# Splitting each mix-matrix strip product of a one-core Trainium2 kernel into two products of 64 output rows in two column tiles

## The chip, the cores and the metric

The kernel runs on one core of one Trainium2 chip. The metric is the device time of one execution in microseconds (us); lower is better. TensorE (PE) does the matrix products, VectorE (DVE), ScalarE (ACT) and GpSimd (POOL) the rest; DMA transfers are issued mostly by SyncE (SP).

## What is computed

The reference is one transformer-like block on 2048 tokens of 1024 features, all float32. Cut to what matters here:

```python
# first half: a mix matrix, kept only where a sparse mask is 1
attn = einsum('ds,td->st', w1, w2) * sparse_mask     # w1, w2, mask: 1024 x 1024
y    = gelu(einsum('bds,st->bdt', x, attn) + b2)
x    = layernorm(x + y)
# second half: weights decoded from bit planes with a 16-entry table per row
x    = layernorm(x + x @ dequant(qweight, lut4).T + bias)   # an 8-bit variant for rows of large norm
```

The mask is 1 only near the diagonal: six-wide windows, shifted by 0, 32 and 64, and their transpose. So of each block of 128 output rows of `attn` only the block itself and at most 69 columns on either side can be nonzero. The kernel rounds that to `REACH = 72` columns.

## The kernel before

**The mix matrix.** The 1024 rows of `attn` are eight blocks `b` of 128. For each block the kernel computes a strip of at most 128 x 272 entries (72 + 128 + 72; 200 columns for the first and the last block, which have only one side) into a PSUM bank, as a sum over eight contraction blocks `d` of 128. The operands `w1` (stationary, 128 columns) and `w2` (moving, up to 272 columns) are plain float32. `strip_row(b, d)` issues one such product; there are 64.

**What is used of a strip.** VectorE's `mask_strip(b)` multiplies the strip by the mask. It takes the middle 128 columns on all 128 rows, the left 72 columns on rows 0 to 63 only and the right 72 columns on rows 64 to 127 only (lines 948, 950 and 953). The few entries beyond that are computed separately by `excess_strip` (line 436), a 48-column product.

**Order.** Each engine runs its instructions in the order written, and semaphores tie the engines together. TensorE does nine warm-up products, then `front_strips()` (`d` outside, blocks 0 to 3 inside), then `back_strips(0)` (blocks 4 and 5) and `back_strips(1)` (blocks 6 and 7). SyncE loads `w1` and `w2` in nine pieces in the same order, and TensorE waits for a piece where it first reads it: five pieces for the front (`d` = 0, 1, 2-3, 4-5, 6-7), then two halves (`d` = 0-3, 4-7) for each pair of back blocks. SyncE waits for nothing in these loads; the masks, the first tokens and part of the bit planes lie between them in its queue.

**What follows.** After the strips TensorE applies the mix matrix to the tokens, group by group (512 tokens): `own(g, t)` is three 512-column products of a diagonal block (lines 475 to 477), `beside(g, t)` three pairs for the blocks beside it, each pair working on partitions 0 to 63 and 64 to 127 (lines 500 and 502), and `excess(g, pair)` (line 487) adds the remaining entries. `own(0, 0)` waits for `make_x_lo(0, 0)` on VectorE (line 1005), and `excess_strip()` is issued after `own(0, 1)`. VectorE's `make_mix_e` (lines 974 to 986) waits for that strip.

VectorE and ScalarE meanwhile decode the weights of the second half (`decode_step`). In VectorE's program the order near the strips' end is `make_x_lo(0, 0)`, `make_x_lo(0, 1)`, `mask_strip(6)`, `make_mix_lo(4)`, `mask_strip(7)`, `make_mix_lo(5)`, `make_mix_e()`. The remaining 240 us are the rest of the first half and the products of the second half (lines 571 to 573).

Of the kernel before, what the change touches and what calls it, by code (L numbers as in the profile page):

```python
# [6 lines left out]
P = 128  # L7
# [6 lines left out]
SIDE = P // 2  # L14
SPAN = STRIDE * (STRIPES - 1)
BITS = 8
REACH = -(-(SPAN + WINDOW - 1) // BITS) * BITS
# [21 lines left out]
def post_ln_block(nc, xt, xr, xe_in, w1d, w1e, w2d, w2e, b2c, mask, mask_b, mask_e, mask_rest, qbits, lut4, lut8, bias, out):  # L39
# [4 lines left out]
    GROUPS, KB = xt.shape[0], xt.shape[1]  # L44
    D = KB * P
# [55 lines left out]
    with ctx:  # L101
# [7 lines left out]
        def at(name, kib, shape, dt):  # L109
            return nc.alloc_sbuf_tensor_at(name, [P] + shape, dt, offset=origin + int(kib * KIB))  # L110
# [3 lines left out]
        w2 = at("w2", 32, [KB, D], f32)  # L114
        w1 = at("w1", 64, [KB, D], f32)
# [71 lines left out]
        def unit_bank(t):  # L187
            return acc[:, UNIT_BANKS[t], :]
# [70 lines left out]
        def strip_of(b):  # L259
            return max(b * P - REACH, 0), min((b + 1) * P + REACH, D)  # L260

        def places_of(b):
            first, end = strip_of(b)
            return slice(first - b * P + REACH, end - b * P + REACH)
# [161 lines left out]
        def _(pe):  # L426
# [11 lines left out]
                last.then_inc(e_made, 1)  # L438

            def strip_row(b, d):  # L440
                first, end = strip_of(b)
                return nc.tensor.matmul(unit_bank(b)[:, places_of(b)], w1[:, d, b * P:(b + 1) * P], w2[:, d, first:end],  # L442
                                        start=d == 0, stop=d == KB - 1)

            def front_strips():
                starts = [first for first, _ in ROW_PIECES]
                for d in range(KB):
                    if d in starts:
                        pe.wait_ge(w_loaded[starts.index(d)], 32)
                    for b in range(FRONT):  # L450
                        last = strip_row(b, d)
                        if d == KB - 1:
                            last.then_inc(mix_made, 1)

            def back_strips(n):
                for d in range(KB):
                    if d % HALF_BLOCKS == 0:
                        pe.wait_ge(w_loaded[len(ROW_PIECES) + 2 * n + d // HALF_BLOCKS], 32)
                    for b in (FRONT + 2 * n, FRONT + 2 * n + 1):
                        last = strip_row(b, d)  # L460
                        if d == KB - 1:
                            last.then_inc(mix_made, 1)
# [184 lines left out]
            with nc.tensor.If(wanted > 0):  # L647
                with pe.Fori(0, KB) as b:
                    with pe.Fori(0, KB) as t:
                        pe.wait_ge(g_w_lo, KB * b + t + 1)  # L650
                        for d in range(KB):
# [3 lines left out]
                            last = nc.tensor.matmul(acc[:, 0, 0:P], lo, g_w_hi[:, 1, d, :], start=False,  # L655
                                                    stop=d == KB - 1)
# [980 lines left out]
```

## Time and profile before

| | |
|---|---|
| median of 3 runs | 298.35 us (298.05 to 298.6) |
| the profiled execution, its own time | 298.25 us |
| its span from the first to the last instruction | 296.4 us |
| TensorE busy in the span | 281.9 us, 95% |
| VectorE busy | 217.9 us, 73% |
| ScalarE busy | 195.7 us, 66% |
| mean granted TensorE clock | 0.99 |
| strip products (line 442) | 64 products, 128 matmul records, from 5.1 to 35.6 us |

How to read it: the profiled execution took 298.25 us from outside, and 296.4 us lie between its first and last instruction. A float32 product leaves two matmul records, each with a weight load of its own, so the 64 strip products are 128 records. The time of one record is a latency, as matmuls are pipelined and their ends are modelled; what a product costs the engine is the distance from one start to the next.

### The profile page before, as it was taken

The page shows a single profiled execution, that of the slowest core. Times are in us where ns is not written, and L with a number is a line of the kernel's source. Part 1 is how long each engine was busy: PE and PEld are TensorE (multiplying, and loading weights), DVE is VectorE, ACT ScalarE, POOL GpSimd, SP SyncE. Part 2 cuts the span into 40 slices and gives each one's busy share as a digit, 9 for nine tenths or more (in the row PEclk, how much of TensorE's full clock was granted, in tenths as well). Part 3 has the DMA queues.
Part 4 walks back from the last instruction along what each step waited for, and adds up shares of the span by engine and source line. Part 5 has one row for each costly group of instructions (what it writes and reads, how often), then busy time and mean ns, then how long its engine had stood idle before and what let it go on. Part 6 is the DMA issues. An engine that isn't in the chain of part 4 may idle for free.

```text
span 296.4 us, 4898 instructions
## 1 busy us (share of the span) xinstructions
PE 281.9 (95%) x1835; PEld 245.8 (83%) x1835; DVE 217.9 (73%) x355; ACT 195.7 (66%) x257; POOL 88.5 (30%) x152
## 2 busy tenths in 40 slices
PE   8899989899999999999999999999999999999980
PEld 4688866667668999999999999999988778888880
DVE  1679999897868977997979686295578586763371
ACT  2866368988999979989989985362447446222110
POOL 4000001533353202121520000000387866766421
PEclk9999999999999999999999999999999999999995
DMA  6999999999999611111111111174188663434323
GB/s 211 400 358 358 377 376 333 246 247 243 205 196 195 138 35 53 38 35 55 35 56 35 45 45 38 54 160 197 64 260 287 226 212 141 140 115 155 123 114 111
DMA packets 28479, 49.76 MB, mean 168 GB/s; under 512 B 2464, under 2 KB 11936, under 8 KB 28448
## 3 DMA queue, kind: packets, MB, share of 16 engines
q1 hardware_dynamic: 23392, 40.53, 40.1%
q0 software_dynamic: 4352, 8.39, 15.8%
q10 hardware_dynamic: 704, 0.46, 0.5%
q8 instruction: 16, 0.26, 0.4%
q14 instruction: 15, 0.12, 0.1%
HBM read 36.79 MB, written 12.58 MB: 167 GB/s over the span
## 4 chain that ended last, share of the span: by engine, by line
PE 60%; ACT 8%; DVE 8%; SPq 7%; DMA 6%; POOL 5%; issue 5%; DVEq 0%; ACTq 0%
PE acc L571 14%; PE acc L573 14%; PE acc L572 14%; PE acc L500 4%; DMA w<-in_w2d 3%; PE acc L475 2%; SPq L286 2%; ACT leaf L745 2%; ACT zz L788 2%; PE acc L510 2%; PE acc L476 2%; PE acc L477 2%; DMA off_band<-in_mask_rest 2%; SPq L285 1%; DVE leaf L1032 1%
## 5 line engine op out<-in xcount | busy, mean ns | idle before, releaser
L571 PE MATMUL acc<-lin,zz 128*128 128x256 f32 (+2 forms) x424 | 130.6, 308 | 0.3 <-issue 0.3
L573 PE MATMUL acc<-lin,zz 128*128 128x256 f32 (+2 forms) x424 | 129.8, 306 | 0.0
L572 PE MATMUL acc<-lin,zz 128*128 128x256 f32 (+2 forms) x424 | 129.5, 306 | 0.0
L571 PEld LDWEIGHTS acc<-lin,zz 128*128 128x128 f32 x424 | 80.1, 189 | 4.5 <-issue 0.5
L572 PEld LDWEIGHTS acc<-lin,zz 128*128 128x128 f32 x424 | 80.2, 189 | 3.9
L573 PEld LDWEIGHTS acc<-lin,zz 128*128 128x128 f32 x424 | 80.0, 189 | 4.1
L745 ACT ACTIVATE leaf<-planes,lut,flip 128x1024 f32<-128x1024 uint8 x56 | 67.5, 1236 | 1.2 <-DVE dest L1032 1.2
L1032 DVE COPY_PREDICATED leaf<-planes,leaf 128x1024 f32<-128x1024 uint8 x32 | 43.5, 1360 | 14.0 <-ACT leaf L745 13.3
L1493 POOL DMA_DIRECT2D z<-in_xr x16 | 19.5, 1224 | 70.8 <-ACT z L727 68.2
L854 ACT ACTIVATE junk<-rows,cols 128x1024 bf16<-128x1024 f32 x15 | 17.2, 1146 | 35.1 <-POOL cols L1467 35.1
L1032 DVE COPY_PREDICATED dest<-planes,leaf 128x1024 f32<-128x1024 uint8 x24 | 32.5, 1356 | 3.7 <-ACT leaf L745 2.3
L442 PE MATMUL acc<-w,w 128*128 128x272 f32 (+1 forms) x128 | 29.3, 389 | 1.2 <-DMA w<-in_w2d 1.2
L442 PEld LDWEIGHTS acc<-w,w 128*128 128x128 f32 x128 | 24.2, 196 | 6.6 <-DMA w<-in_w2d 2.8
L1465 POOL TENSOR_TENSOR cols<-cols 128x1 f32<-128x1 f32 x15 | 6.8, 455 | 67.0 <-DVE rows L1152 66.9
L1074 DVE TENSOR_TENSOR zz<-z,zz 128x1024 fp32r<-128x1024 f32 x16 | 19.3, 1222 | 7.6 <-ACT zz L788 7.6
L1152 DVE SCALAR_TENSOR_TENSOR rows<-acc,cols,bias_bc 128x512 f32<-128x512 f32 x15 | 11.2, 750 | 17.1 <-PE acc L573 16.9
L727 ACT ACTIVATE z<-acc,b 128x512 f32<-128x512 f32 x32 | 20.3, 692 | 4.2 <-PE acc L502 4.2
L1443 POOL TENSOR_SCALAR cols<-parts 128x1 f32<-128x1 f32 x16 | 9.7, 609 | 41.3 <-ACT parts L838 41.3
L838 ACT ACTIVATE parts<-acc 128x258 f32<-128x258 f32 (+1 forms) x32 | 12.1, 377 | 12.8 <-PE acc L573 12.7
L1005 DVE TENSOR_TENSOR x_lo<-z,x_hi 128x1024 fp32r<-128x1024 f32 x16 | 19.0, 1222 | 0.3
L1157 DVE TENSOR_SCALAR rows<-rows,cols 128x1024 f32<-128x1024 f32 x15 | 12.2, 813 | 8.9 <-POOL cols L1474 8.8
L843 ACT ACTIVATE off_band<-off_band 128x896 f32<-128x896 f32 x8 | 7.6, 952 | 15.1 <-DMA off_band<-in_mask_rest 15.1
(118 smaller groups left out, 438.4 us busy)
## 6 DMA issues: line engine op xcount, KB each, us to landing
z<-in_xt SPq DMA_DIRECT2D x16, 512.0 KB, 8.7
z<-in_xr POOLq DMA_DIRECT2D x16, 512.0 KB, 8.5
out_rows<-rows SPq DMA_DIRECT2D x15, 512.0 KB, 2.9
out_rows<-parts SPq DMA_DIRECT2D x32, 128.0 KB, 1.7
rows<-out_rows SPq DMA_DIRECT2D x16, 256.0 KB, 2.7
w<-in_w1d SPq DMA_DIRECT2D x7, 512.0 KB, 9.0
off_band<-in_mask_rest SPq DMA_DIRECT2D x8, 448.0 KB, 4.7
w<-in_w2d SPq DMA_DIRECT2D x3, 584.0 KB, 9.5
```

The lines of the kernel that those rows point to most:

```text
L442: return nc.tensor.matmul(unit_bank(b)[:, places_of(b)], w1[:, d, b * P:(b + 1) * P], w2[:, d, first:end], start=d == 0, stop=d == KB - 1)
L571: nc.tensor.matmul(bank, hi, w_hi, start=k == 0, stop=False)
L572: nc.tensor.matmul(bank, hi, w_lo, start=False, stop=False)
L573: last = nc.tensor.matmul(bank, lo, w_hi, start=False, stop=k == KB - 1)
L727: nc.scalar.activation(z[:, g, t, :], unit_bank(t), ACT.Gelu, bias=b2[:, t:t + 1]).then_inc(gelu_done, 1)
L745: nc.scalar.activation(to, planes[:, b % 2, 0, :], ACT.Identity, bias=lut[:, b, 2 * i:2 * i + 1], scale=flip[:, b, i:i + 1]).then_inc(leaf ...
L854: nc.scalar.activation(junk[:, :], rows[:, j % 4, :], ACT.Square, bias=neg_mean2[:, j:j + 1], accum_out=sq2[:, j:j + 1]).then_inc(squared2, 1)
L1005: nc.vector.tensor_tensor(x_lo[:, 2 * r:2 * r + 2, :], z[:, g, 2 * r:2 * r + 2, :], x_hi[:, 2 * r:2 * r + 2, :].bitcast(f32), ALU.subtract ...
L1032: nc.vector.copy_predicated(to, planes[:, b % 2, plane, :], leaf[:, other, :]).then_inc(merged, 1)
L1074: nc.vector.tensor_tensor(zz[:, 0, g, 2 * r:2 * r + 2, :], z[:, g, 2 * r:2 * r + 2, :], zz[:, 1, g, 2 * r:2 * r + 2, :].bitcast(f32), ALU. ...
L1157: nc.vector.tensor_scalar(rows[:, j % 4, :], rows[:, j % 4, :], neg_mean2[:, j:j + 1], rstd2[:, j:j + 1], ALU.add, ALU.mult).then_inc(norm ...
L1493: nc.gpsimd.dma_start(z[:, g, 2 * r:2 * r + 2, :], xr[g, 2 * r:2 * r + 2].rearrange("k p n -> p k n"), accum_op=ALU.add).then_inc(residual ...
```

## The change

`strip_row` issues two products where it issued one. The first has the weight columns 0 to 63 of the block, writes PSUM partitions 0 to 63, and streams the block's own 128 columns and the 72 to the left. The second has weight columns 64 to 127, writes partitions 64 to 127, and streams the own 128 columns and the 72 to the right. The output partitions place them in the two 64-column tiles of the 128-column array. The corner regions that no longer are computed (rows 64 to 127 of the left 72 columns, rows 0 to 63 of the right 72) are those that `mask_strip` does not read.

```diff
             def strip_row(b, d):
-                first, end = strip_of(b)
-                return nc.tensor.matmul(unit_bank(b)[:, places_of(b)], w1[:, d, b * P:(b + 1) * P], w2[:, d, first:end],
-                                        start=d == 0, stop=d == KB - 1)
+                for rows_, low, high in ((slice(0, SIDE), REACH, 0), (slice(SIDE, P), 0, REACH)):
+                    first, end = max(b * P - low, 0), min((b + 1) * P + high, D)
+                    to = unit_bank(b)[rows_, first - b * P + REACH:end - b * P + REACH]
+                    half = w1[:, d, b * P + rows_.start:b * P + rows_.stop]
+                    last = nc.tensor.matmul(to, half, w2[:, d, first:end], start=d == 0, stop=d == KB - 1)
+                return last
```

The order of TensorE's program shows it. In the rows below `acc` is the PSUM, `w_51` and `w_52` are the two weight matrices in SBUF, the size is output partitions by streamed columns, and `w_loaded5` to `w_loaded8` are the landings of the last four pieces of the weights. First `back_strips(0)` and the start of `back_strips(1)` in the kernel before:

```order
 L442 MATMUL acc<-w_51,w_52 128x272 [waits w_loaded5]
 L442 MATMUL acc<-w_51,w_52 128x272 x7
 L442 MATMUL acc<-w_51,w_52 128x272 [waits w_loaded6]
 L442 MATMUL acc<-w_51,w_52 128x272 x7
 L442 MATMUL acc<-w_51,w_52 128x272 [waits w_loaded7]
 L442 MATMUL acc<-w_51,w_52 128x200
```

The same place in the changed kernel:

```order
 L445 MATMUL acc<-w_51,w_52 64x200 [waits w_loaded5]
 L445 MATMUL acc<-w_51,w_52 64x200 x15
 L445 MATMUL acc<-w_51,w_52 64x200 [waits w_loaded6]
 L445 MATMUL acc<-w_51,w_52 64x200 x15
 L445 MATMUL acc<-w_51,w_52 64x200 [waits w_loaded7]
 L445 MATMUL acc<-w_51,w_52 64x200 x2
 L445 MATMUL acc<-w_51,w_52 64x128
```

The eight products behind each landing have become sixteen, and the two halves of a product stand one behind the other. Then the end of the strips on the same engine, where `own(0, 0)`, `own(0, 1)` and `excess_strip` follow, in the kernel before:

```order
 L442 MATMUL acc<-w_51,w_52 128x200
 L475 MATMUL acc<-x_hi,mix_hi 128x512 [waits x_lo_made,mix_lo]
 L476 MATMUL acc<-x_lo,mix_hi 128x512
 L477 MATMUL acc<-x_hi,mix_lo 128x512
 L475 MATMUL acc<-x_hi,mix_hi 128x512 [waits x_lo_made,mix_lo]
 L476 MATMUL acc<-x_lo,mix_hi 128x512
 L477 MATMUL acc<-x_hi,mix_lo 128x512
 L436 MATMUL acc<-w_e 128x48 [waits masked,e_ld]
```

And in the changed kernel, where lines after the edit are 3 higher:

```order
 L445 MATMUL acc<-w_51,w_52 64x200 x3
 L445 MATMUL acc<-w_51,w_52 64x128
 L478 MATMUL acc<-x_hi,mix_hi 128x512 [waits x_lo_made,mix_lo]
 L479 MATMUL acc<-x_lo,mix_hi 128x512
 L480 MATMUL acc<-x_hi,mix_lo 128x512
```

What follows the strips waits for the same semaphores as before, and nothing but the strips' own products has changed. In all there are 128 strip products instead of 64, 112 of 200 columns and 16 of 128.

## Rows read from the trace of the kernel before

**Rows 1.** The page: span, TensorE's busy time, and the chain that ended last, by engine.
```profile
span 296.4 us, 4898 instructions
PE 281.9 (95%) x1835; PEld 245.8 (83%) x1835; DVE 217.9 (73%) x355; ACT 195.7 (66%) x257; POOL 88.5 (30%) x152
...
PE 60%; ACT 8%; DVE 8%; SPq 7%; DMA 6%; POOL 5%; issue 5%; DVEq 0%; ACTq 0%
```

**Rows 2.** The chain that ended last, 20 to 45 us: start, us, what.
```profile
22.28 9.81 DMA w<-in_w2d
...
32.13 3.46 PE acc L442 x16
...
37.00 1.73 PE acc L436 x16
```

**Rows 3.** Timeline of TensorE: start, us to the last end, records, idle before.
```profile
5.86 1.11 PE L442 MATMUL acc<-w,w 128*128 128x272 f32 x2
...
7.20 0.62 PE L442 MATMUL acc<-w,w 128*128 128x272 f32 x2
...
10.76 0.60 PE L442 MATMUL acc<-w,w 128*128 128x200 f32 x2 [0.86 <-DMA w<-in_w2d]
...
12.57 0.50 PE L442 MATMUL acc<-w,w 128*128 128x200 f32 x2
...
20.68 0.62 PE L442 MATMUL acc<-w,w 128*128 128x272 f32 x2
...
32.13 3.46 PE L442 MATMUL acc<-w,w 128*128 128x272 f32 x16 [0.31 <-DMA w<-in_w2d]
```

**Rows 4.** Loads of weights: the chain's issue rows, and DMA windows holding one issue each.
```profile
5.34 0.60 SPq L279
...
w<-in_w2d SPq DMA_DIRECT2D x1, 584.0 KB, 11.1
...
17.62 2.30 SPq L286
...
w<-in_w2d SPq DMA_DIRECT2D x1, 368.0 KB, 9.4
```

**Rows 5.** Timeline of VectorE, 20 to 40 us.
```profile
20.54 0.37 DVE L948 TENSOR_TENSOR mix_raw<-acc,band 128x128 f32<-128x128 f32 x1 [0.95 <-DMA band<-in_mask_b]
...
34.00 2.36 DVE L1005 TENSOR_TENSOR x_lo<-z,x_hi 128x1024 fp32r<-128x1024 f32 x2
...
38.04 0.40 DVE L960 TENSOR_TENSOR mix_lo<-mix_raw,mix_hi 128x256 fp32r<-128x256 f32 x1
38.76 0.26 DVE L974 TENSOR_TENSOR raw_e<-acc,band_e 128x96 f32<-128x96 f32 x1 [0.32 <-PE acc L436]
```

**Rows 6.** All waits of VectorE, 20.9 to 40 us: total, times, longest.
```profile
DVE mix_raw L948 <- DMA band<-in_mask_b: 1.0, 1, 1.0
DVE raw_e L974 <- PE acc L436: 0.3, 1, 0.3
```

**Rows 7.** Groups of TensorE and its weight loads, 0 to 75 us, shapes apart: busy us, mean ns.
```profile
L442 PE MATMUL acc<-w,w 128*128 128x272 f32 x96 | 25.2, 401 | 0.3 <-DMA w<-in_w2d 0.3
...
L436 PE MATMUL acc<-w_e 128*128 128x48 f32 x16 | 1.9, 271 | 0.0
...
L442 PEld LDWEIGHTS acc<-w,w 128*128 128x128 f32 x128 | 24.2, 196 | 6.6 <-DMA w<-in_w2d 2.8
```

**Rows 8.** Timeline of TensorE, 61 to 66 us: pairs on partitions 0-63 and 64-127.
```profile
61.51 0.40 PE L500 MATMUL acc<-x_hi,mix_lo 64*128 64x512 f32 x1
61.51 0.39 PE L502 MATMUL acc<-x_hi,mix_lo 64*128 64x512 f32 x1
61.75 0.39 PE L500 MATMUL acc<-x_hi,mix_hi 64*128 64x512 f32 x1
```

**Rows 9.** The chain that ended last, 61 to 66 us, across a change of tiling.
```profile
62.60 0.43 PE acc L475
63.03 0.23 PE acc L476
```

## The prediction

> **What bounds the kernel now.** I read the page first. The last-ended chain is 60% TensorE, and TensorE is busy for 95% of the span [rows 1]: a microsecond lost on it early is likely lost for good. Whether one gained early is kept must be read where the strips end, so next came the chain from 20 to 45 us [rows 2]. It does not run through the strips of the front. It runs through SyncE's queue to the last piece of `w2`, issued at 22.28 and landed at 32.09 us, then through the 16 records behind that piece (3.46 us), `own` and the 16 records of `excess_strip` to `make_mix_e`. The reader is to see that transfers, not products, set when the last quarter of the strips may start.
>
> Third, TensorE's timeline [rows 3]. Before the last piece TensorE waited only 0.31 us (it was busy to 31.82), and before the piece landing at 10.7 us it waited 0.86 us. In between it was dense. So strips and transfers are nearly balanced: faster strips run into landings, much slower ones soon move the end.
>
> Fourth, VectorE [rows 5, 6]. From 20.9 to 38.4 us it does not wait for a strip at all; its first `mask_strip` waited for the mask's transfer (to 20.54), and it waits for TensorE only once, 0.32 us at 38.76, for `excess_strip`. `make_x_lo(0, 0)`, which `own(0, 0)` needs, is the first half of the pair from 34.00 to 36.36, so it ends near 35.2.
>
> **What a product costs now.** Two 272-column records at 20.68 cover 0.62 us; less one record's latency (0.39, [rows 7] has a mean of 0.401) their starts are 0.229 apart. For 200 columns: 0.50 - 0.33 = 0.169 [rows 3]. Difference: 0.060 us for 72 columns, 0.83 ns a column; so a record is 0.0025 + 0.00083 x columns. With two records a product: 272 columns 0.458 us, 200 columns 0.338, 128 columns 0.218. Behind the last landing stand four products of 272 and four of 200: 4 x (0.458 + 0.338) = 3.19 us, and a restart after the wait of about 0.10 (32.13 + 3.46 less the last latency 0.33 gives the last start, 35.26; the 15 steps make 3.02 of the 3.13 between). So the strips leave the engine at 32.13 + 0.10 + 3.19 = 35.42.
>
> **The change, part by part.**
>
> *Streams.* An inner block's 0.458 becomes two products of 0.338 on different halves of the array. No row of this kernel shows column tiles. Bounds: from below, they run at once and a block costs 0.338; from above, one after the other, 0.677. The nearest rows are the `beside` pairs [rows 8]: two records on partitions 0-63 and 64-127 start in the same 10 ns, and the next pair 0.24 later, the price of one. Those are row tiles of one record each. Here a half has two records, A1 A2 B1 B2 in program order. If starts are in order and a tile holds one stream, B1 starts with A2, and B2 with the next A1: four records in two slots of 0.169. I take 0.338, since the overlap of tiles is the nearest row. The end blocks cost 0.338 either way (200 and 128 columns at once), as before. The Trainium skill, TensorEngine Tiling (Array Packing), Key Properties, says that tiles can load and multiply in parallel, and TensorE: Matmul & The Clock Gate, Part 3, gives 2.38 times for three column tiles; no run here shows it.
>
> *Weight loads.* 128 loads become 256 of half the columns. The dearest price in sight is that of `excess_strip`, whose 48-column records are too short to hide a load: 1.73 us for 16 [rows 2], 0.108 each. Four at full price would be 0.43 a block, four at half price 0.22. Now 128 loads (24.2 us busy) lie under products of the same 128 rows, for the starts are 0.229 apart with loads of 0.196 [rows 7]. I take them as hidden, cost 0; if their price does not halve, the cover of 0.338 is gone and a block costs 0.43.
>
> *Change of tiling.* After pairs of 64 rows, the first record of 128 rows takes 0.43 us in the chain, the next 0.23 [rows 9]: 0.20 for the change. One is added on the path, strips to `own(0, 0)`; the one from warm-up to strips lies ahead of landings TensorE waits for anyway.
>
> *The sum.* At once, front blocks cost 4 x 0.338 = 1.35 a `d`. The front's last piece lands at 5.34 + 11.1 = 16.4 [rows 4], so the front ends at 16.4 + 2.7 = 19.1, still ahead of the mask at 20.5 for which VectorE waits. The third back piece lands at 17.62 + 9.4 = 27.0; its eight products end at 27.0 + 8 x 0.338 = 29.7. The last piece lands at 32.1 as before, since SyncE issues it behind no engine. Then 32.13 + 0.10 + 2.71 = 34.94, 0.48 earlier than 35.42. But `own(0, 0)` needs its tokens at 35.2, so it starts then, with a change of tiling that lies partly under the wait: first stream at about 35.2 to 35.4, a gain of 0 to 0.2, say 0.1. Nothing behind can return more, as VectorE's slack at `excess_strip` is 0.32 and its program is dense to 38.44. So 5.8 us less of TensorE work (48 blocks x 0.12) is worth 0.1 us. Sum: 298.25 - 0.1 = 298.15; the profiled execution was 0.1 below the median of 298.35, so the forecast is 298.2.
>
> **The rivals.**
>
> *Halves do not overlap.* In favour: no row shows two records of one product's kind at once, each half brings two records of its own tile in a row, and both tiles read the same 128 partitions, where the row tiles each read their own 64. Against: [rows 8]. Then inner blocks cost 0.677 and end blocks 0.338 + 0.218 = 0.556. TensorE falls behind from the second piece on: the first `d` at the early half rate (two 272-column records at 5.86 cover 1.11 us, starts 0.45 apart, 0.23 from 7.2 on, [rows 3]) ends near 8.7, the second 2.59 later at 11.3; then 6 x (0.556 + 3 x 0.677) = 15.5 to 26.8, back blocks 4 and 5 16 x 0.677 = 10.8 to 37.6, blocks 6 and 7 8 x (0.677 + 0.556) = 9.9 to 47.5, with the tiling change 47.7: 12.3 later than 35.42. VectorE, dense but only 18 us of work after the first mask, is done earlier, so all of it shows: 298.35 + 12.3 = 310.6. This is the rival on the other side; it decides from about 0.468 a block on (from 10.76 + 0.10, 56 blocks of cost c must end by 35.4, 14 of them end blocks and 0.12 cheaper each: 56c - 1.7 = 24.5), and every 0.01 beyond costs 0.56 us.
>
> *Weight loads become the bound.* Four of 0.108, 0.43 for every block, the end blocks too: 32.23 + 8 x 0.43 = 35.7, with the change of tiling 35.9, 0.45 later: 298.8, at the edge of what can be told. For: double the loads; against: they have half the columns.
>
> *Loads that can't lie under products.* Then 0.338 + 0.43 = 0.77 a block: 10.86 + 56 x 0.77 = 54.0, plus 0.2, 18.8 later: 317. Against it speaks that 0.196 us loads already hide. The page TensorE: Matmul & The Clock Gate of the Trainium skill, Part 3, says that a weight load overlaps products in flight only when its row group differs, and two column tiles share theirs; the trace of before disagrees for this kernel, as its loads of all 128 rows hide.
>
> *The clock falls.* At once, TensorE would stand idle from 29.7 to 32.1, 2.4 us, where its longest pause among the strips is now 0.86 [rows 3], and the mean granted clock of the span is 0.99. If the lower level (1.2 of 2.4 GHz) came back, 0.45 against 0.229 a record, the last eight products would cost 5.4 instead of 2.7 and end at 37.6, with the tiling change 37.8: 2.4 later, 300.7. For: the strips start at that level, in spite of the nine warm-up products ahead of them. Against: a pause of 0.86 did nothing.
>
> **How the numbers follow.** At once, loads hidden, clock kept: 0.60. Load-bound: 0.07. Clock: 0.06. No or little overlap: 0.24. Exposed loads: 0.03. The likeliest has its own range of 297.8 to 298.7: the gain can't pass 0.3, to which the run's spread of 0.3 is added. A change of 0.2%, 0.6 us, is what a measurement of this kernel can tell from none. Same: nearly all of the first case and half of the load-bound one, 0.58; faster by more 0.05, if something is freed that I don't see; slower 0.37. The range must reach the case without overlap, as it holds over 2 in 10: 297.8 to 311.0; it leaves out only the exposed loads.
>
> **What would show it.** Right: 256 strip records, 128 starts of them beside another, mean distance 0.085 us; TensorE idle before the second to fourth back pieces, above all about 2.4 us before 32.1; `own(0, 0)` within 0.2 us of before; VectorE's program unmoved. Wrong: starts 0.169 apart without idle time and strips that end near 47 us; starts 0.11 apart (loads); records twice as far apart after 32.1 (clock); or a last landing that is not at 32.1. The forecast fails outright if column tiles don't overlap with two-record float32 products; a partial overlap up to 0.468 a block would leave it standing.

## The result and the profile after

The changed kernel took 299.5 us (median of 19 runs, 298.52 to 301.31), the kernel before 298.7 (19 runs, 297.97 to 299.8): 0.8 us slower between the medians. The ratio of the means is 1.003 (0.9 us) with a 95% interval of 1.0017 to 1.0043. The profiled execution took 299.01 us. The forecast was 298.2 and "same" the likeliest.

The page of the changed kernel, against [rows 1]: TensorE has 6 us less to do, and the span is 0.8 us longer.

```profile
span 297.2 us, 5154 instructions
PE 275.8 (93%) x1963; PEld 240.8 (81%) x1963; DVE 218.0 (73%) x355; ACT 195.6 (66%) x257; POOL 88.6 (30%) x152
...
PE 58%; DVE 11%; ACT 8%; DMA 6%; POOL 5%; issue 5%; SPq 3%; DVEq 0%; ACTq 0%
```

**The halves do overlap.** TensorE's timeline after, against [rows 3]; the columns are those of [rows 3].

```profile
20.91 0.85 PE L445 MATMUL acc<-w,w 128*64 128x200 f32 x8
...
28.28 2.53 PE L445 MATMUL acc<-w,w 128*64 128x200 f32 x28
32.82 2.92 PE L445 MATMUL acc<-w,w 128*64 128x200 f32 x32 [2.01 <-DMA w<-in_w2d]
36.58 0.47 PE L478 MATMUL acc<-x_hi,mix_hi 128*128 128x512 f32 x1 [0.83 <-DVE x_lo L1008]
```

The 28 records from 28.28 cover 2.53 us; less one latency of 0.33 that is 2.20 for 13 steps of 0.169, two records a step (the row of eight at 20.91 gives 0.52 for three). So a block of four records costs 0.338 us. The 32 records behind the last piece take 2.92 us where 16 took 3.46. The price on which the forecast rested is right.

**But the end of the strips came later.** The last piece landed at 32.8, not at 32.1, TensorE had stood idle for 2.01 us, and `own(0, 0)` started at 36.58 instead of 35.4, because it waited for VectorE's `make_x_lo`. VectorE's timeline and all its waits say why, against [rows 5] and [rows 6]:

```profile
21.73 0.38 DVE L951 TENSOR_TENSOR mix_raw<-acc,band 128x128 f32<-128x128 f32 x1 [2.03 <-DMA band<-in_mask_b]
...
35.21 2.36 DVE L1008 TENSOR_TENSOR x_lo<-z,x_hi 128x1024 fp32r<-128x1024 f32 x2
...
39.96 0.26 DVE L977 TENSOR_TENSOR raw_e<-acc,band_e 128x96 f32<-128x96 f32 x1 [0.32 <-PE acc L436]
```

The first `mask_strip` started at 21.73 instead of 20.54, and every VectorE instruction from there to `raw_e` is 1.19 to 1.23 us later than before. This is the whole shift: TensorE's wait for VectorE, the wait at `raw_e` (0.32 in both) and the groups behind it keep their distances. It lasts: SyncE issues the last store at 291.86 us instead of 290.56, 1.30 later. Of that 0.8 is left in the span, so in this pair of profiles the end behind the last store took 0.5 us less. The reader is to see that the lateness enters at one instruction, which waits for the mask transfer and for nothing of TensorE's.

**Why the mask was late.** Three views: transfers from 18.0 to 18.1 us of the changed kernel, transfers from 24.6 to 24.8 us of the kernel before, and the mask's own issue, after and before (us from issue to landing in the last column).

```profile
q1 hardware_dynamic: 31, 0.04, 113.4%
q8 instruction: 1, 0.02, 72.4%
```
```profile
q1 hardware_dynamic: 80, 0.06, 109.6%
q8 instruction: 1, 0.02, 37.2%
```
```profile
band<-in_mask_b SPq DMA_DIRECT2D x1, 400.0 KB, 11.2
```
```profile
band<-in_mask_b SPq DMA_DIRECT2D x1, 400.0 KB, 10.2
```

Beside the data the DMA engines carry the instructions: a packet of 16 KB on queue 8. By the packets' own records it starts at 24.66 us and takes 1.19 us before, and starts at 18.05 us and takes 1.16 us after. A transfer lands in 16 parts. Those of the mask, from the landing records (us):

```
before  15 from 19.26 to 20.42, the last 20.52
after   15 from 19.39 to 20.51, the last 21.70
```

Fifteen parts are in time, one is late by the length of the read. The same happens to the small transfer of the bit planes (15 by 20.94, one at 22.14) and holds up SyncE's queue (the issue at 17.71 takes 3.46 us, 2.30 before), and the pieces of the weights behind the read land late too (20.65, 25.14, 27.75 and 32.78 against 19.43, 23.91, 26.99 and 32.09). That the last piece is late because of the read is read from these times; no run tests it alone. Before, the read came behind the mask's landing.

### The profile page after: what moved, and what is told of

Same layout as the page of the kernel before. It is cut to its first block, busy times and chain, and to the rows that moved or that the text cites. A ratio compares the mean times of both kernels' runs of the same rounds, so it can differ in the third digit from the quotient of the medians.

```text
span 297.2 us, 5154 instructions
## 1 busy us (share of the span) xinstructions
PE 275.8 (93%) x1963; PEld 240.8 (81%) x1963; DVE 218.0 (73%) x355; ACT 195.6 (66%) x257; POOL 88.6 (30%) x152
## 4 chain that ended last, share of the span: by engine, by line
PE 58%; DVE 11%; ACT 8%; DMA 6%; POOL 5%; issue 5%; SPq 3%; DVEq 0%; ACTq 0%
PE acc L574 14%; PE acc L576 14%; PE acc L575 14%; DMA band<-in_mask_b 4%; PE acc L503 4%; PE acc L478 2%; ACT leaf L748 2%; DVE leaf L1035 2%; ACT zz L791 2%; PE acc L513 2%; PE acc L479 2%; PE acc L480 2%; DMA off_band<-in_mask_rest 2%; PE acc L557 1%; DVE dest L1035 1%
## 5 line engine op out<-in xcount | busy, mean ns | idle before, releaser
L445 PE MATMUL acc<-w,w 128*64 128x200 f32 (+1 forms) x256 | 23.3, 329 | 7.6 <-DMA w<-in_w2d 7.5
L445 PEld LDWEIGHTS acc<-w,w 128*64 128x64 f32 x256 | 19.3, 137 | 11.8 <-DMA w<-in_w2d 10.5
L1077 DVE TENSOR_TENSOR zz<-z,zz 128x1024 fp32r<-128x1024 f32 x16 | 19.3, 1224 | 7.7 <-ACT zz L791 7.7
```

The source lines that it names most:

```text
L445: last = nc.tensor.matmul(to, half, w2[:, d, first:end], start=d == 0, stop=d == KB - 1)
L1077: nc.vector.tensor_tensor(zz[:, 0, g, 2 * r:2 * r + 2, :], z[:, g, 2 * r:2 * r + 2, :], zz[:, 1, g, 2 * r:2 * r + 2, :].bitcast(f32), ALU. ...
```

## The experiments

Each run also has a mean granted clock, and these told more than one profile. The changed kernel: 7 of 19 runs at 0.990 or more, with a median of 298.89; 12 at 0.982 to 0.986, with 299.89. The kernel before, beside the experiments: 30 of 35, 28 of 35 and 23 of 29 runs at 0.990 or more, with medians of 298.68, 298.60 and 298.37. So the profiled execution shows one cause, and most runs have a second.

What the mean says must be read from the clock records of the profiles. In each of them the clock is at its lower level from 290 to 295 us to the end, for 2.9 to 6.0 us; this alone makes a mean of 0.990 to 0.995. Four of the 13 profiles hold one more stretch at the lower level, each 3.41 us long, which takes another 0.006. So a run at 0.986 or less very likely lost the clock somewhere before the end, and one at 0.987 to 0.989 may or may not have. The mean does not say where the clock fell.

Two theories, which may add up: the instruction read moves ahead of the mask; the granted clock falls behind the pause of 2 us. The rival to both: column tiles or the change of tiling cost something by themselves.

All eleven kernels had 12 runs each; "high" counts those at 0.990 or more, "low" those at 0.986 or less. By the same count the changed kernel had 12 of 19 low, and the kernel before 0 of 35, 0 of 35 and 2 of 29. The runs came from three chips, and the changed kernel itself was not run again beside them, so a comparison with its 299.5 or 298.89 is one across sessions; the high runs of the kernel before alone differ by 0.3 us between them.

| run | median us | before, same chip | ratio (95%) | high | median of high | low |
|---|---|---|---|---|---|---|
| after_warm1 | 299.38 | 298.68 | 1.0018 (1.0000 to 1.0036) | 3 | 298.66 | 6 |
| before_tiny25 | 298.71 | 298.68 | 0.9995 (0.9976 to 1.0013) | 11 | 298.69 | 0 |
| after_band_first | 298.86 | 298.68 | 0.9999 (0.9971 to 1.0027) | 3 | 298.40 | 5 |
| split_back_only | 300.49 | 298.68 | 1.0060 (1.0035 to 1.0085) | 2 | 298.13 | 7 |
| after_fill | 298.98 | 298.64 | 1.0000 (0.9980 to 1.0019) | 12 | 298.98 | 0 |
| split_back_fill | 300.72 | 298.64 | 1.0065 (1.0035 to 1.0095) | 4 | 299.57 | 5 |
| split_back_band_fill | 298.61 | 298.64 | 1.0005 (0.9984 to 1.0026) | 10 | 298.57 | 0 |
| before_narrow | 299.15 | 298.64 | 1.0018 (0.9990 to 1.0046) | 6 | 298.39 | 5 |
| before_tiny44 | 298.85 | 298.38 | 0.9995 (0.9972 to 1.0019) | 12 | 298.85 | 0 |
| after_band_fill | 298.69 | 298.38 | 1.0012 (0.9978 to 1.0046) | 8 | 298.36 | 3 |
| split_back_fill8 | 298.60 | 298.38 | 0.9997 (0.9971 to 1.0023) | 9 | 298.29 | 1 |

**after_warm1**, to move the read back:

```diff
-    WARM_UP = 9
+    WARM_UP = 1
```

> The changed kernel with 1 warm-up product instead of 9, so TensorE's program reaches every later point 8 products sooner. Theory (instruction read): in the changed kernel a 16 KB packet of the instruction queue starts at 18.05 us, takes 1.16 us, and one of the 16 parts of the mask transfer lands at 21.70 while the other 15 are in by 20.51; VectorE is late by 1.20 us from there to the end. With 8 products fewer ahead of it the read should start behind the front's 64 products, after 20 us, the mask should land at 20.5, and the time should be 0.9 to 1.3 us below the changed kernel, at about the kernel before. Rival (transfers vary by themselves, or the column tiles slow them): the mask still lands near 21.7 and the time is that of the changed kernel. Rival (the 1.2 us come from the change of tiling or a lower clock): no gain, and a loss if fewer warm-ups lower the clock of the front.

A miss on where the read falls: it started at 18.13, and the first `mask_strip` at 21.11. Eight bf16 warm-up products are too few instructions to move it past the front. But its profile, at a mean clock of 0.985, caught the second cause. The windows of this run (the columns are the length, TensorE, its weight loads, VectorE, ScalarE and GpSimd busy, then the granted clock, the share of the DMA engines and GB/s):

```profile
30.00:32.00 2.00, 0.17 (x2) 0.00 (x0) 1.96 (x9) 0.68 (x2) 0.00 (x0) 1.00 1.12 368
32.00:34.00 2.00, 1.71 (x13) 1.59 (x15) 1.92 (x6) 1.42 (x4) 0.00 (x0) 0.63 1.01 376
34.00:36.00 2.00, 2.00 (x17) 1.74 (x14) 1.97 (x3) 0.92 (x1) 0.00 (x0) 0.51 1.06 392
36.00:38.00 2.00, 2.00 (x15) 1.47 (x12) 1.92 (x5) 0.25 (x1) 0.00 (x0) 1.00 1.08 362
```

TensorE stands idle from 30 to 32.3 us; then the granted clock is at the lower of its two levels (1.2 of 2.4 GHz) until about 36, and the last 32 records take 4.60 us instead of 2.92. `own(0, 0)` starts at 36.82 and `raw_e` at 40.23, 1.47 later than in the kernel before; 0.57 of this is the late mask, so the fallen clock cost 0.9 us. The Trainium skill, TensorE: Matmul & The Clock Gate, in its part on HAM oscillation, says that waits for transfers between bursts of products bring the half rate back. This trace agrees, after a wait of 2.12 us; the profiles of `after`, `after_band_first`, `split_back_only` and `before_narrow` have waits of 2.0 to 2.1 us at the same place and no fall behind them.

**before_tiny25**, to pull the read forward in a kernel without column tiles:

```diff
-    WARM_UP = 9
+    WARM_UP = 4
...
+            for _ in range(25):
+                nc.tensor.matmul(acc[:, SUM_BANK, 0:8], warm[:, 0:P], warm[:, 0:8], start=True, stop=True)
```

> The kernel before with 4 warm-up products and 25 products of 8 columns instead of 9 warm-up products: 20 more products in TensorE's program, the strips untouched. Theory (instruction read): the read that starts at 24.66 us in the kernel before is pulled ahead of the mask's landing at 20.5, one part of the mask lands about 1.2 us late, VectorE's first mask_strip starts near 21.7, and the kernel is about 1.2 us slower (0.4%) without any column tile. Rival (column tiles or faster strips are the cause): the mask lands at 20.5 and the time is that of the kernel before within 0.2%.

A miss: the read moved from 24.66 to 20.36, still too late to touch the mask (20.54 in both), and the time stayed. It shows that the length of TensorE's program places the read, and that added products cost nothing by themselves.

**after_band_first**, to take the mask out of the read's way:

```diff
-            load_back(0, 0)
             load_band(0)
+            load_back(0, 0)
```

> The changed kernel with the first mask half (band) loaded ahead of the first back piece of the weights instead of behind it. Theory (instruction read): the mask lands near 17.5 to 18.7, so the read no longer delays VectorE's first mask_strip, which starts when the decode step ahead of it is done, near 19.7; but the read still delays the later transfers, so the last piece of weights lands near 32.8, the strips end near 35.6, and own(0, 0) starts near 35.8 instead of 36.6: 0.6 to 1.0 us faster than the changed kernel, about the kernel before. Rival (the 1.2 us arise in the strips themselves): nothing changes.

As expected by the read: the first `mask_strip` starts at 19.35, `own(0, 0)` at 35.17, `raw_e` at 38.60 (39.96 in the changed kernel, 38.76 in the kernel before), and the median is 0.6 us below the changed kernel's and 0.2 above that of before on its chip. The last piece came at 32.3, better than expected. Only 3 of 12 runs kept the high clock. One of the other nine took 452.59 us at a mean clock of 0.558; it is not in the ratio, and it has no trace.

The profiled execution (299.36 us, 0.989) lost its clock, but not behind the pause of 2.06 us ahead of the last piece. Its windows (columns as above):

```profile
243.00:244.00 1.00, 1.00 (x5) 0.74 (x4) 1.00 (x2) 0.62 (x1) 0.95 (x1) 0.54 0.73 252
244.00:245.00 1.00, 1.00 (x4) 0.80 (x3) 1.00 (x2) 1.00 (x3) 0.00 (x0) 0.50 0.99 401
```

The store that SyncE issues at 242.77, as in the kernel before (242.72), is the last in time; the one that came at 254.64 comes at 256.21. So a fall here costs 1.5 us. TensorE had been idle for 0.87 us ahead of 240.72 (0.64 in the kernel before, whose clock stayed, and 0.90 in before_tiny44, whose clock stayed too).

**split_back_only**, one part of the change alone:

```diff
+                if b < FRONT:
+                    first, end = strip_of(b)
+                    return nc.tensor.matmul(unit_bank(b)[:, places_of(b)], w1[:, d, b * P:(b + 1) * P], w2[:, d, first:end],
+                                            start=d == 0, stop=d == KB - 1)
```

> Only the products of blocks 4 to 7 are split; blocks 0 to 3 are whole as in the kernel before. Theory (instruction read): TensorE's program ahead of the first back piece is that of the kernel before, so the read starts no earlier than that piece's landing at 19.5, at 20 to 21 us; the mask lands at 20.5 and the time is within 0.1% of the kernel before, perhaps 0.1 us faster, unless the read just touches the mask's last part (then up to 1.2 us slower). Rival (column tiles cost on the path, as the change of tiling ahead of own(0, 0)): as slow as the changed kernel, 0.9 us above before.

The read starts at 25.22, the mask lands at 20.44, and the two runs at 0.990 take 298.04 and 298.21 us, like before. The ten others take 300.8 in the median. So a run with a fallen clock is 2.7 us slower here and 1.0 in the changed kernel. This is the larger effect, which I had not expected of this run. Why it is larger is open, as no such run of this kernel was profiled. In the changed kernel VectorE's lateness of 1.2 us could hide part of a fall behind the last piece; but such a fall made the strips only 1.7 us longer in after_warm1, less than the 2.7 here, so more than that is in these ten runs. A fall near 243 us (1.5 us in after_band_first) and the late store of split_back_fill below are candidates.

**after_fill**, to take away the pause alone:

```diff
+            def fill(pairs, alone):
+                for _ in range(pairs):
+                    for rows_ in (slice(0, SIDE), slice(SIDE, P)):
+                        nc.tensor.matmul(unit_bank(KB - 1)[rows_, 288:488], w1[:, 0, rows_], w2[:, 0, 0:200],
+                                         start=alone, stop=alone)
...
                 for d in range(KB):
+                    fill({(1, 4): 6}.get((n, d), 0), d == 0)
```

> The changed kernel with six more pairs of 64-row products (2.0 us of TensorE work, into unused columns of a bank) ahead of the wait for the last piece of the weights, in the pause of 2.1 us. Theory (clock): in most executions of the changed kernel the granted clock halves behind that pause; with the pause filled the mean clock should be 0.99 or more in nearly all runs, their time about that of the changed kernel's runs at 0.99 or more (298.9), so 0.5 to 0.9 us below its median of 299.5. What the instruction read costs stays, 0 to 0.4 us above before. Rival (the read alone makes the 0.9 us): the time stays 299.5, with the clock as before.

All 12 runs kept 0.990 or more, against 7 of 19, and the median is 298.98: 0.5 below the changed kernel's and near that of its high runs (298.89). Against the kernel before on the same chip the ratio is 1.0000, where it was 1.003. TensorE's timeline shows the filled pause (line 461 is the filler):

```profile
30.23 2.31 PE L461 MATMUL acc<-w,w 128*64 128x200 f32 x23
32.57 2.92 PE L445 MATMUL acc<-w,w 128*64 128x200 f32 x32
36.27 0.47 PE L485 MATMUL acc<-x_hi,mix_hi 128*128 128x512 f32 x1 [0.78 <-DVE x_lo L1015]
```

More work on TensorE made the kernel faster. The fillers also change the places of the later reads (one at 227.02 instead of 232.86), so that the pause alone made the difference is likely, not shown. The wait for `x_lo` of 0.78 us, which the read causes (at 18.74, first `mask_strip` at 21.42), is left, and so are 0.3 us against before by the medians (298.64).

**before_narrow**, the same speed of the strips without a column tile and without one instruction more. The right 72 columns of the inner strips are left incomplete from the second contraction block on.

```diff
                 first, end = strip_of(b)
-                return nc.tensor.matmul(unit_bank(b)[:, places_of(b)], w1[:, d, b * P:(b + 1) * P], w2[:, d, first:end],
+                if d and 0 < b < KB - 1:
+                    end -= REACH
+                to = unit_bank(b)[:, first - b * P + REACH:end - b * P + REACH]
+                return nc.tensor.matmul(to, w1[:, d, b * P:(b + 1) * P], w2[:, d, first:end],
```

> The kernel before with whole 128-row products, but the inner blocks stream only 200 columns from the second contraction block on; the right 72 columns of their strips are left incomplete. So a product costs 0.338 us as in the changed kernel, with no column tile and not one instruction more. Theory (clock): the same pauses as in the changed kernel, so the clock falls below 0.99 in more than half of the runs and the median is 0.3 to 2 us above before, while the instruction read starts at 24 us or later and the mask lands at 20.5. Rival (column tiles or the added instructions are the whole cause): clock and time as before, or 0.1 us faster.

TensorE's timeline has the same pause ahead of the last piece:

```profile
27.24 3.09 PE L445 MATMUL acc<-w,w 128*128 128x272 f32 x16 [0.26 <-DMA w<-in_w2d]
32.33 2.97 PE L445 MATMUL acc<-w,w 128*128 128x200 f32 x16 [2.00 <-DMA w<-in_w2d]
```

Six of 12 runs fell below 0.990 and took 300.1 in the median, the others 298.39; the read was at 23.50, the mask on time. Five of the six are at 0.986 or less, against none of the 35 of the kernel before on the same chip. So neither tiles nor instructions are needed for the clock to fall: faster strips, with the pauses that they bring, are enough. Over all runs the loss (ratio 1.0018, 0.9990 to 1.0046) is not clear of noise, and the one profile is of a run without a fall, so the place of the falls is not seen.

**before_tiny44**, the read alone:

```diff
-    WARM_UP = 9
+    WARM_UP = 1
...
+            for _ in range(44):
+                nc.tensor.matmul(acc[:, SUM_BANK, 0:8], warm[:, 0:P], warm[:, 0:8], start=True, stop=True)
```

> The kernel before with 1 warm-up product and 44 of 8 columns instead of 9: 36 products more ahead of the strips, where before_tiny25 had 20 more and its read started at 20.36, just too late to touch the mask. Counting two instructions for a small product and four for a float32 one, the read should now start between the landings of the fourth and fifth front piece, at 16.5 to 19 us. Theory (instruction read): one part of the mask then lands about 1.2 us late, the first mask_strip starts near 21.7, raw_e near 40.0 instead of 38.8, and the kernel is 0.9 to 1.3 us slower than before with its clock unchanged (0.99). Rival (the read costs nothing by itself, the mask was late by chance): mask at 20.5, time as before within 0.2%.

The read came where it was computed to come, at 17.78. VectorE's timeline:

```profile
21.02 0.38 DVE L950 TENSOR_TENSOR mix_raw<-acc,band 128x128 f32<-128x128 f32 x1 [1.27 <-DMA band<-in_mask_b]
```

The mask was late by 0.48 us, not by 1.2, and `raw_e` by 0.44. All 12 runs kept the clock, and their median is 298.85 against 298.37 of before's high runs: 0.48 us, the same number. The ratio over all runs does not tell this apart, since 6 of before's 29 runs were below 0.990. So the read costs by itself; how much depends on how late the part that it delays would have been, 0.5 to 1.2 us in these profiles (0.57, 0.88 and 1.19 with the changed strips).

**after_band_fill**, both causes treated: after_band_first with `fill({(0, 0): 5, (0, 4): 1, (1, 4): 6}.get((n, d), 0), n == 0 or d == 0)`.

> The changed kernel with both causes treated: the first mask half ahead of the first back piece, so the read at 18 us no longer delays VectorE's start, and 5, 1 and 6 pairs of filler products ahead of the three waits with pauses. If the two causes add up to the whole loss: nearly all runs at a clock of 0.99 or more, median 298.2 to 298.6, 0.9 to 1.3 us below the changed kernel and 0 to 0.15% below the kernel before. If something else costs too: above 298.8.

Eight runs at 0.990 or more have a median of 298.36, just that of before (298.37), 0.5 below the changed kernel's. Four runs were at 0.981 to 0.988 and took over 301, so the fillers do not cover every place, and the median of 298.69 is above the range expected. Treating both causes brings back the time of before only in the runs that keep the clock.

**split_back_fill**, **split_back_fill8** and **split_back_band_fill**: split_back_only with fillers of `{(1, 4): 6}`; of `{(1, 0): 2, (1, 4): 6}`; and the latter with the mask first.

> Blocks 4 to 7 split as in split_back_only, with the same six pairs ahead of the wait for the last piece. Theory (clock): two of split_back_only's twelve runs kept the clock at 0.99 and took 298.0 and 298.2 us, ten were at 0.980 to 0.989 and took 300.2 to 303.3. Filled, nearly all runs should be like those two: 298.1 to 298.4, 0.1 to 0.2% faster than before. Rival (the slow runs have another cause, such as transfers): median still near 300.5. If the lower clock starts behind the 1 us pause ahead of the piece before, only half of it is regained.

> As split_back_fill, with the first mask half loaded ahead of the first back piece, and two more pairs ahead of the third back piece. Expected to beat both kernels: VectorE's first mask_strip starts near 20.0, when the first strip is done, instead of 20.5, and TensorE leaves the strips at 35.1, so at most 0.3 us below split_back_fill: 297.8 to 298.2, 0.2% to 0.3% faster than before. Rival (clock falls all the same): 299 to 300.5.

> split_back_fill with two more filler pairs ahead of the third back piece, the mask's place untouched. In split_back_fill's profile a read of instructions starts at 213.74 us, 0.5 us behind a store whose landing the next reload waits for, and that store takes 3.98 us; in split_back_band_fill the read starts at 212.3. Theory (reads at other places cost too): two pairs more move the read back to about 212.3, the time falls from 300.7 to 298.5 to 298.9 and most runs keep 0.99. Rival (split_back_fill was slow for another reason, such as the mask's place): still 300 or more.

The first is a miss: 300.72, 8 of 12 runs below 0.990, though the pause ahead of the last piece is filled. In its profile the strips end as before (`raw_e` at 38.91), but near 225 us it is 1.3 us late, behind a store issued at 213.22 that takes 3.98 us, and at 243.5 us the clock falls for 3.4 us. The other two, with four 64-row products more, are at 298.6 with 9 (split_back_fill8) and 10 high runs. That is as expected for split_back_fill8. For split_back_band_fill it is a miss: 297.8 to 298.2 was expected, and it does not beat the kernel before. Yet the one profile of split_back_fill8 (a run of 0.988) shows 0.9 us of lateness near 225 us and the fall too, with its read at 212.57; and after_band_first has the fall without that lateness. Ahead of the fall TensorE had waited 1.73 us for VectorE in split_back_fill and 1.43 in split_back_fill8, at a place where it waits 0.53 to 0.92 us in the other eleven profiles, after_band_first's 0.87 among them. So what tips the later stretch is not settled; that it lies near 213 to 245 us, and that a few instructions more or less ahead of it change how often, is all that was seen.

## Why the prediction was wrong

- **Streams**: right. "I take 0.338" was measured as 0.338; two records start within 7 ns and the next two 0.17 us later. Of the Trainium skill's rules named there, the trace agrees with the one that tiles load and multiply in parallel. It does not agree with the one that a weight load overlaps only products of another row group: 256 loads lie under products of the same rows, and no start is later for it.
- **Weight loads**: right, hidden; 19.3 us busy in 256 loads.
- **The pauses**: right ahead of the last piece (2.01 us against 2.4), though both its ends moved: 30.8 to 32.8 instead of 29.7 to 32.1. One was expected ahead of the third back piece too and did not come, since the second piece landed at 25.14 and its products lasted beyond the third's landing at 27.75.
- **The sum**: its failed step is "The last piece lands at 32.1 as before, since SyncE issues it behind no engine", and with it the mask's landing at 20.5, which it took as fixed. Both were read as bound by SyncE's queue and the DMA engines alone. But instructions come through the same engines, 16 KB at a time (that these are TensorE's follows from before_tiny25 and before_tiny44, where more products moved the read), and 64 products more, run earlier, moved such a read from 24.66 to 18.05 us, ahead of the one transfer for which VectorE waits. The last piece landed at 32.8, the mask at 21.7, and with it the tokens that were needed at 35.2 came at 36.4. In place of "a gain of 0 to 0.2", `own(0, 0)` was 1.2 us late in the profiled execution. Over the high-clock runs the read cost about 0.3 us (298.89 against 298.4 to 298.7 in the three other sessions; 298.98 against 298.60 in after_fill's own), which is little beside the noise.
- **The clock falls**: the second step that failed is "Clock: 0.06". In 12 of 19 runs the mean clock was 0.982 to 0.986, with a loss of 1.0 us in their median. "A pause of 0.86 did nothing" says nothing about one of 2. The mechanism was written down with its place, and after_warm1's profile shows it there; how many of the 12 falls lay there is not seen, as the changed kernel's own profile has none and three other profiles have theirs near 243 us. The price of 2.4 us was too high: the clock was low for 3.41 us only, the last products took 1.7 us longer instead of 2.7, and 0.9 of it reached `raw_e`.
- **How the numbers follow**: the interval held the median, but "same" was the likeliest and the case that came was split over rivals that were priced one at a time. Two small losses from the same gain, faster strips, were not considered together: 0.3 of the read and 0.6 of the clock (12 of 19 runs, 1.0 us each) make the 0.9.
- **The overall gain** of 0.1 us is smaller than the times can tell: after_band_fill's high runs are at before's (298.36 and 298.37). In after_band_first's profile `raw_e` comes 0.16 us earlier than before and the stores up to 213 us 0.19, so a gain of that size was there, with the mask loaded first, until the clock fell.

No version here beats the kernel before by more than the measurement can tell. split_back_only's two high runs (298.04 and 298.21 against 298.68) are the lowest, but its other ten make it the second slowest of all.

## What to carry to other kernels

Making an engine faster ahead of a landing that it waits for turns work into a pause; on TensorE ask what the pause does to the clock of the work behind the landing, before counting the change as free. Where a transfer is on the chain, know when instruction reads come: adding instructions to TensorE moved them here, and one 16 KB packet held up one of the sixteen parts of each transfer in flight. And look at the clock of every run beside its time: one profile showed only one of the two causes. But a mean clock has no place in it; profile a run that lost the clock before saying where it was lost.

## What was not expected of the hardware

- A read of 16 KB of instructions took 0.9 to 1.3 us in most cases, and in the saturated start one part of a transfer landed 1.2 us behind the other fifteen.
- Two float32 products on the two 64-column tiles, two records each in a row, ran at full overlap (0.338 us a pair), also where the tiles read the same 128 partitions.
- One program kept TensorE's clock in 7 of its 19 executions and lost some of it in the other 12. In the profiles a fall lasted 3.41 us each time, once behind a pause of 2.12 us, and three times near 243 us.
